# Zero and one fills of a two-layer decoder kernel: done by GpSimd in place of VectorE

## The reference

```python
x = x + L0_attn(layernorm(x))            # causal self-attention
x = x + L0_xattn(layernorm(x), ctx)      # cross-attention on 77 rows
x = x + L0_ffn(layernorm(x))             # 8 linear experts, 2 chosen
x = x + L1_attn(layernorm(x))            # a recurrence: h = tanh(x_t Wi + bi + h Wh + bh), 1024 steps
x = x + L1_xattn(layernorm(x), ctx)      # cross-attention with biases
x = x + L1_ffn(layernorm(x))             # 16 gated experts, 4 chosen, and a shared one
```

## Time and profile before

| | |
|---|---|
| median of 3 runs | 1412.26 us (1410.08 to 1412.88) |
| the profiled execution's own time | 1410.35 us |
| its span | 1408.3 us |
| mean granted TensorE clock | 0.977 of full |
| TensorE matmul (PE) busy | 1353.7 us, 96% |
| VectorE (DVE) busy | 849.8 us, 60%, 2678 instructions |
| ScalarE (ACT) busy | 630.1 us, 45% |
| GpSimd (POOL) busy | 39.4 us, 3%, 60 instructions |
| chain that ended last, by engine | PE 90%, DVE 5%, DMA 1%, ACT 1%, issue 1% |

### The profile page before, as it was taken

One profiled execution on the slowest core, in us unless ns is written; L12 is line 12 of the kernel. 1 busy time (PEld: TensorE's weight loads), 2 busy tenths in 40 slices (PEclk: granted clock), 3 DMA queues, 4 the chain that ended last, 5 costly groups with the idle time before them and its releaser, 6 DMA issues.

```text
span 1408.3 us, 48623 instructions
## 1 busy us (share of the span) xinstructions
PE 1353.7 (96%) x19876; PEld 918.5 (65%) x19876; DVE 849.8 (60%) x2678; ACT 630.1 (45%) x2842; POOL 39.4 (3%) x60
## 2 busy tenths in 40 slices
PE   4798979999999999999999999999999999999998
PEld 2455436777756777776577777766667776765654
DVE  6757774268775225979661225758555565447585
ACT  2163304833524784253248876553253435433422
POOL 2000000000000000000000000000000000000000
PEclk9899989999999999999999999989999999989999
DMA  5746100021000002110000003310000200001000
GB/s 139 122 124 128 37 1 3 3 50 16 3 2 3 3 3 34 40 34 3 2 3 3 3 3 108 81 30 2 2 2 3 55 3 3 17 3 39 2 16 15
DMA packets 45471, 40.20 MB, mean 29 GB/s; under 512 B 9723, under 2 KB 44486, under 8 KB 45254
## 3 DMA queue, kind: packets, MB, share of 16 engines
q1 hardware_dynamic: 42662, 35.53, 11.1%
q10 hardware_dynamic: 2592, 1.57, 0.9%
HBM read 25.81 MB, written 10.80 MB: 26 GB/s over the span
## 4 chain that ended last, share of the span: by engine, by line
PE 90%; DVE 5%; DMA 1%; ACT 1%; issue 1%; SPq 0%; DVEq 0%; ACTq 0%
PE b L515 23%; PE b L1654 9%; PE b L534 8%; PE b L1431 6%; PE b L1023 6%; PE b L994 5%; PE b L1722 5%; PE b L939 4%; PE b L696 3%; DVE mx L948 3%; PE b L1300 3%; PE b L1275 2%; PE b L744 2%; PE b L459 2%; PE b L651 2%; PE b L501 1%
## 5 line engine op out<-in xcount | busy, mean ns | idle before, releaser
L515 PEld LDWEIGHTS b<-hp,whp 128*128 128x128 f16 x12276 | 472.1, 96 | 255.1 <-ACT hp L560 168.6
L515 PE MATMUL b<-hp,whp 128*128 128x2 f16 x12276 | 532.5, 165 | 1.0
L566 DVE TENSOR_TENSOR hp<-hist,hp 128x4 f16<-128x4 f32 x1023 | 164.5, 161 | 405.6 <-ACT hist L561 394.9
L560 ACT ACTIVATE hp<-b 128x4 f16<-128x4 f32 x1024 | 178.0, 174 | 442.8 <-PE b L515 430.2
L948 DVE TENSOR_REDUCE mx<-b 128x1 f32<-128x512 f32 (+3 forms) x304 | 189.9, 652 | 0.5 <-PE b L939 0.3
L1008 ACT ACTIVATE vp<-b 128x512 f32<-128x512 f32 x288 | 171.7, 603 | 17.7 <-PE b L997 9.8
L561 ACT ACTIVATE hist<-b 128x4 f32<-128x4 f32 x1024 | 177.2, 173 | 0.0
L534 PE MATMUL b<-whp 128*128 128x512 f16 (+6 forms) x608 | 162.1, 342 | 0.0
L1654 PE MATMUL b<-vp,heads 128*128 128x512 f16 x576 | 160.5, 380 | 0.0
L939 PE MATMUL b<-heads 128*128 128x512 f16 (+3 forms) x384 | 113.1, 333 | 5.8 <-DVE mx L948 2.8
L1431 PE MATMUL b<-we,xT 128*128 128x512 f16 x384 | 106.0, 383 | 0.0
(11 more groups left out here) (220 smaller groups left out, 1620.7 us busy)
## 6 DMA issues: line engine op xcount, KB each, us to landing
x_qs<-qx_scr SPq DMA_DIRECT2D x42, 128.0 KB
qx_scr<-xq_pair SPq DMA_DIRECT2D x16, 256.0 KB, 2.1
heads<-q_scr SPq DMA_DIRECT2D x24, 128.0 KB, 5.0
heads<-k_scr SPq DMA_DIRECT2D x36, 64.0 KB, 2.8
x<-in_x SPq DMA_DIRECT2D x8, 256.0 KB, 6.7
q_scr<-tail SPq DMA_DIRECT2D x8, 256.0 KB, 2.3
k_scr<-tail SPq DMA_DIRECT2D x8, 256.0 KB, 2.3
x_qs<-in_L_ffn_We SPq DMA_DIRECT2D x2, 1024.0 KB, 6.2
```

Source lines behind the costliest of these rows:

```text
L515: return pe.matmul(self.z(t)[:, m], self.w.whp[:, a, k, m * P:(m + 1) * P], self.g.hp16[:, (t - 1) % 2, part, k, :], start=False, stop=Tru ...
L560: act.activation(self.g.hp16[:, t % 2, 0], self.z(t), ACT.Tanh, scale=1 / LIFT).then_inc(self.s["hi_ready"], 1)
```

## The change

All 19 fills of `fill`, `zero` and `one` are given to the engine "pool" (GpSimd) in place of "v" (VectorE). The semaphores, the waits in the functions and the ranks are the same. The costs that are given to the planner are larger. Other fills (L97, L570, L1630, L2032, L2035) stay on VectorE.

```diff
-        st.add("v", name + "_zero", self.zero, 2, 1.4, early, behind=first)
-        st.add("v", name + "_one", self.one, 4, lambda i: (0.5, 1.2, 1.2, 0.5)[i], lambda i: early(i // 3), behind=first + weights)
+        st.add("pool", name + "_zero", self.zero, 2, 1.6, early, behind=first)
+        st.add("pool", name + "_one", self.one, 4, lambda i: (0.8, 1.4, 1.4, 0.8)[i], lambda i: early(i // 3), behind=first + weights)
...
-    def zero(self, v, layer):
+    def zero(self, pool, layer):
         if layer:
-            self.over(v)
-        v.memset(self.layers[layer].ks_words, 0.0).then_inc(self.s["zeroed"], 1)
+            self.over(pool)
+        pool.memset(self.layers[layer].ks_words, 0.0).then_inc(self.s["zeroed"], 1)
...
-    def one(self, v, i):
+    def one(self, pool, i):
...
-                v.wait_ge(*self.queries_free)
-            v.memset(self.qs[:, half * (i - 1):half * i].rearrange("p h n -> p (h n)").bitcast(F32), ONES16
+                pool.wait_ge(*self.queries_free)
+            pool.memset(self.qs[:, half * (i - 1):half * i].rearrange("p h n -> p (h n)").bitcast(F32), ONES16
...
-        def fill(v, i):
+        def fill(pool, i):
...
-                v.memset(heads[:, 8192 + 2048 * (i - 3):8192 + 2048 * (i - 2)], 0.0).then_inc(s["filled"], 1)
+                pool.memset(heads[:, 8192 + 2048 * (i - 3):8192 + 2048 * (i - 2)], 0.0).then_inc(s["filled"], 1)
...
-        st.add("v", "fill", fill, 5 + B * NK, lambda i: 0.2 if i < 3 else 2.0 if i < 5 else 1.1,
+        st.add("pool", "fill", fill, 5 + B * NK, lambda i: 0.4 if i < 3 else 2.2 if i < 5 else 1.3,
                lambda i: 1.0 if i < 3 else 10.12 if i < 7 else 70.0,
                behind=[("qk_part2", lambda i: 4 if i >= 7 else 0)])
```

More of the change, by code:

```diff
@@ L1096, in one @@
             if i:
-                self.over(v)
-            v.memset(w.vc.rearrange("p b w -> p (b w)"), 1.0).then_inc(self.s["oned"], 1)
+                self.over(pool)
+            pool.memset(w.vc.rearrange("p b w -> p (b w)"), 1.0).then_inc(self.s["oned"], 1)
         else:
@@ L2014, in router @@
                                        ).then_inc(s["wr_split"], 1)
-        def fill(v, i):
+        def fill(pool, i):
             if i == 0:
-                v.memset(rw.lift_row[:], LIFT).then_inc(s["filled"], 1)
+                pool.memset(rw.lift_row[:], LIFT).then_inc(s["filled"], 1)
             elif i == 1:
-                v.memset(wx0.ones16[:], 1.0).then_inc(s["filled"], 1)
+                pool.memset(wx0.ones16[:], 1.0).then_inc(s["filled"], 1)
             elif i == 2:
-                v.memset(wx1.one_row[:], 1.0).then_inc(s["filled"], 1)
+                pool.memset(wx1.one_row[:], 1.0).then_inc(s["filled"], 1)
             elif i < 5:
-                v.memset(heads[:, 8192 + 2048 * (i - 3):8192 + 2048 * (i - 2)], 0.0).then_inc(s["filled"], 1)
+                pool.memset(heads[:, 8192 + 2048 * (i - 3):8192 + 2048 * (i - 2)], 0.0).then_inc(s["filled"], 1)
             else:
                 c, b = (i - 5) // B, (i - 5) % B
-                v.memset(heads[:, 4096 * b:4096 * (b + 1)].rearrange("p (r t) -> p r t", r=H // 2)[
+                pool.memset(heads[:, 4096 * b:4096 * (b + 1)].rearrange("p (r t) -> p r t", r=H // 2)[
                     :, :, P * c:P * (c + 1)], ONES16).then_inc(s["filled"], 1)
```

## The result

| | before | after |
|---|---|---|
| median of 11 runs | 1411.65 us (1407.6 to 1420.15) | 1426.77 us (1412.85 to 1443.65) |
| ratio after / before | | 1.0087, 95% interval 1.0058 to 1.0115 |
| span of the profiled execution | 1408.3 us | 1419.7 us |
| mean granted TensorE clock in it | 0.977 | 0.970 |

The kernel got slower by 0.87%, where 1407.1 us and a gain were forecast. The runs of the kernel after also lie further apart.

What follows compares the result with a forecast made beforehand. PE, busy 1050.61 of 1052 us in the recurrence, was the bound, so its start had to gain. Gains of 3.1 + 1.3 + 0.8 = 5.2 us took the profiled 1410.35 to 1405.15; adding 1.91 gave 1407.1, range 1400 to 1416.

Steps and rivals of the forecast that it cites:

- What starts it earlier by a microsecond ends it earlier by one: Recurrence, 220 to 1272 us: fixed matmul work keeps PE busy, so an earlier start moves its end equally.
- another deal: Rival: the planner orders the recurrence's stretch otherwise; slower at 1415.5 us, chance 0.20, or its mirror at 1401, chance 0.06.
- the sum: Likeliest case, chance 0.55: gains of 3.1, 1.3 and 0.8 us, together 5.2, giving 1407.1 us.
- the same 1188: Sign of being right: from the first L515 to the end the kernel still takes 1188 us.
- The price of another deal: Recurrence: 5% more of PE's 168.6 us of weight-load waits for ScalarE's tanh, costing 8.4 us.
- The slower rival: Planner's new order adds waiting for tanh in the recurrence: 1407.1 + 8.4 = 1415.5 us, chance 0.20.
- 24 to 55 us, gain 3.1: Before the recurrence: chunk 1's moments gain 2.2 us, zeroing `x_ks` 0.9; `lift` moves from 53.73 to about 50.6.
- six fills between 39.85 and 45.0: VectorE fills holding PE for most of 6.25 us; moving them was priced at zero, PE waiting for `lift` anyway.
- 108 to 135 us, gain 2.1: Moving the `x_qs` fills lets moments run earlier, 1.3 us; moving layer 1's zeroing and ones gains 0.8.
- Price on GpSimd: A 128x1024 fill costs 0.9 to 1.8 us on GpSimd, taken as 1.2; 128x2048 costs 1.8 to 3.6.
- The hold on GpSimd: Rival: at chunk 1 and the cross norm, powers or normalisings wait for fills; 3.8 us lost, 1410.9 us, chance 0.12.
- What would show it wrong: Signs: 128x1024 fill over 2 us, held power or normalising, `lift` still 53 to 54, L515 stretch over 3 us from 1052.

Runs made afterwards that it cites:

- e9: The kernel after, unchanged, run again beside another kernel on the same chip; 1426.44 us, ratio 1.0108 to before.
- e1: The kernel before with its written order kept and only the 19 fills moved to GpSimd at their planned times; 1410.92 us, ratio 0.9994.
- e7: The kernel before's order with the fills on GpSimd, plus two waits putting fills behind normalisings; 1410.72 us, ratio 0.9994.
- e10: Second run of the kernel after with the kernel before's fill costs given to the planner; 1421.36 us, ratio 1.0048.
- e2: The kernel after with its written order kept and the 19 fills set back on VectorE; 1432.01 us, ratio 1.0124.
- e4: First run of the kernel after with the kernel before's fill costs given to the planner; 1416.83 us, ratio 1.0022.

## Why the prediction was wrong, point by point

- *"What starts it earlier by a microsecond ends it earlier by one, as long as the planner deals the work in much the same way."* This condition is the step that failed. I read "same ranks, same amount of work" as "much the same order", gave another deal 0.20 for slower and 0.06 for faster, and treated it as noise around the sum. The order was new from TensorE's first entry. The planner is greedy and its pieces hang together, so taking 19 pieces off one engine's list moved most of what stands behind them. In the place of a start 5.2 us earlier and a stretch of 1052 us, the profile showed a start 0.8 us later (6.9 us in the second profile, e9) and a stretch of 1067.8 us (1068.1). From the first L515 to the end it took 1198.4 us, not "the same 1188".
- *The price of another deal* had the wrong currency. I had 5% more waiting for tanh, 8.4 us. The waiting for tanh rose only from 168.6 to 174.9 us. The other idle time of L515's weight loads rose as well, `issue` from 13.9 to 19.3 and the subtraction L566 from 0.6 to 5.0 us, but the blocks above show no loss from any of it at full clock: 977.2 and 977.4 us over the same 49 of 52 blocks. What the new order brought was time at half clock: 41 us more in the profile, at 0.347 us each 14.2 of the 15.8 us. Over all runs it is 28.8 us more (91.7 against 62.9), by the lines 9.5 to 11.2 of the 14.7 us between the means. The rest is not assigned; a later start is the likely part of it. The row that could have warned me is in the earlier trace rows: 0.99 and not 1.00, and 0.977 on the page. The kernel before spent 27 us at half clock in a stretch where PE reads as busy without a pause, and I never priced it. The slower rival ended at 1415.5 and the range at 1416, 11 us under the result.
- *24 to 55 us, gain 3.1.* Tested alone in the old order (e1), `lift` came at 51.8 instead of 53.73: 1.9 us; with the waits of e7 51.5. The step had the right sign, and was too large. Its overlap was wrong: of the 4.2 us that leave VectorE most were not in the way of the moments. In e1 VectorE waits there for ScalarE's parts (2.39 and 0.60 us), and the moments start at 27.80, only 1.2 us earlier, so the turn comes at 30.92, 1.1 us earlier and not 2.2, with PE still idle for 1.14 us. `load_q` was issued at 35.20 (e7: 34.90), where 33 to 34 was forecast. I also counted six fills between 39.85 and 45.0, and there are five, the sixth is at 37.25; the term was nothing either way. In after itself the order of ScalarE and SP was other: the key loads were issued at 50.42 on ScalarE, ahead of `lift`, which came at 57.29, 3.6 us later than before.
- *108 to 135 us, gain 2.1.* Not seen as such. The recurrence of e1 starts at 219.5, 1.0 us earlier than before, less than `lift` had gained; that of e7 starts 2.7 us earlier, 0.5 more than `lift` had gained (2.2). For all steps 5.2 was forecast.
- *Price on GpSimd.* Right, and on the cautious side: 1.03 us, estimate 1.2. The upper end of 1.8 us, a factor of two over VectorE, isn't what a fill costs here: the factor is 1.13 for 128x1024 and 1.02 for 128x2048.
- *The hold on GpSimd* was a rival with 0.12, at up to 1.9 us for each normalising. The mechanism is real, and larger: up to 7.0 us over eight fills back to back, though in two of the six profiles with the new order and fills on GpSimd (after, e10) VectorE came in behind the third fill, after 2.5 us. It is also a part of why VectorE's busy time fell by 7.7 and not by 16.4 us: time spent held counts as busy, and the 16 normalisings of chunks' first norm went from 6.1 to 10.9 us together, 4.8 of the missing 8.7. The other 3.9 are no hold: in e7, where nothing is held, VectorE's busy time is 837.3 us, 12.5 less than before and again 3.9 short of 16.4. Added up one by one, VectorE's rows fall by 11.7 us in the kernel after, just 16.4 less 4.8. Neighbouring rows overlap by some 0.1 us, and the busy time of the page counts such time once. By the rule cited in the prediction (the Trainium skill, SBUF — State Buffer, Who interferes with whom) the second comer is blocked for the whole instruction; the trace agrees, and goes beyond it, as the 7.02 us span eight fills. In the old order the end doesn't feel it (e1 against e7: the same ratio); in the new order the two pairs of profiles above leave 5 to 6 us at the start open.
- *What would show it wrong* named the right view: a stretch from first to last L515 off by over 3 us. It was off by 15.8.

What stays open: why the new order lets the clock fall more often. In it, falls come back near 595 to 645, 870, 900, 975, 1110 to 1160 and 1230 us, in each of four profiles (after twice, e2, e10) at most of these places; in the old order mostly near 890, 925 and 1235. In the 10 us ahead of the first six falls of the kernel after TensorE read as busy for 9.4 to 10.0 us. Ahead of four of them it had 32 to 39 matmuls of 64 columns or more, where 47 is the median of the recurrence, but ahead of those at 599 and 971 it had 65 and 49. Stretches with as few of them stand in many places without a fall, and no experiment here changed one such place by itself. The half clock in the whole run also differs from run to run of one kernel, 34 to 91 us in before, which says that where it falls isn't fixed by the program alone. That the amount goes with the order within the recurrence is shown by the five and four profiles and the mean of all runs; which trait of that order does it is not. The start may have a part too: e4 and e10, with after's recurrence and another start, have 78 us in the whole run on average, between before and after. Why isn't shown.

## What to carry to other kernels

Where a program's order is written by a planner, an edit to one engine, cost or count can be an edit to all of it: first compare the written orders, and if one effect is to be measured, freeze the order and move the one thing. Price the clock before the waits: half-clock time times its rate (here 0.35 us for each us) can be larger than any gain that such an edit has to offer, and it hides behind a PE that is 100% busy. A fill on GpSimd is about as fast as on VectorE and takes load off it (12.5 us in e7), but keep it clear of VectorE work like these normalisings.

## What the hardware showed that I had not expected

- A 128x256 normalising on VectorE, 0.41 us alone, lasted 7.02 us beside eight fills on GpSimd without a pause (e4), and 2.54 us beside the same fills in another profile of the same kernel (e10). In the old order its longest, 1.58 us, was at 0.41 us again when the fills waited for it (e1, e7). Its time held counts as busy.
- A large memset costs GpSimd 1.03 us for 128x1024 and 1.79 for 128x2048, 13% and 2% above VectorE.
- Runs of the same program spread over 20 us (before: 1401.65 to 1421.28), and the time goes with that at half clock, with a correlation of 0.93. Outside such spans the recurrence repeats closely: 42 blocks of 20 steps agree to 0.06 us each between two profiles (after and e4).
- In steps whose weight load waits 0.3 us or more, a filler matmul of 384 columns still costs 0.14 us of the chain. Such a wait is not all free time.
